# Mixture-of-experts layers of a one-core kernel: the rows of six sequences sorted by expert and run in 55 blocks of 128

## The reference

```python
scores = sigmoid(xf @ gate_w + bias)                # 4096 rows, 8 experts
top_scores, top_idx = top_k(scores, 2)
top_scores = top_scores / (sum(top_scores) + 1e-06)
w = zeros((T, E)).at[arange(T)[:, None], top_idx].add(top_scores)
up = einsum('th,ehi->tei', xf, up_w) + up_b         # h = 128, i = 512
hact = gelu(up)
eo = einsum('tei,eih->teh', hact, down_w) + down_b
combined = einsum('teh,te->th', eo * 0.1, w)
shared = (gelu(xf @ sw_up + sb_up) @ sw_down + sb_down) * 0.1
out = shared + combined
out = out / (max(abs(out), axis=-1) + 1e-06)        # then x = x + 0.5 * out
```

## Time and profile before

| | us |
|---|---|
| median of 3 runs | 1536.26 (1531.91 to 1538.03) |
| the profiled execution | 1536.07 |
| its span in the trace | 1534.3 |
| PE busy | 1386.0, 90% |
| DVE busy | 946.8, 62% |
| ACT busy | 800.9, 52% |
| POOL busy | 400.0, 26% |

### The profile page before, as it was taken

How to read it: one execution, slowest core, us unless ns; L and a number is a source line. 1 busy time by engine, 2 the same in 40 slices (tenths; PEclk the granted TensorE clock), 3 DMA queues, 4 the chain that set the end, 5 groups by cost and what they waited for, 6 DMA issues and landing times. The chain is left out here.

```text
span 1534.3 us, 24908 instructions
## 1 busy us (share of the span) xinstructions
PE 1386.0 (90%) x8338; PEld 725.6 (47%) x8338; DVE 946.8 (62%) x1898; ACT 800.9 (52%) x1465; POOL 400.0 (26%) x585
## 2 busy tenths in 40 slices
PE   2896999999999789799999996998998879999997
PEld 1771222222222268577777763221221257777776
DVE  5687788888889357441222274899999941222236
ACT  0221788888878624344434354656765444443432
POOL 3122233231231022300000003788887700000000
PEclk9995899999999989699999997899999979999999
DMA  4020222122221010000000002444444200000001
GB/s 95 2 84 1 73 74 74 41 72 75 73 73 33 2 19 2 1 16 16 1 16 17 1 1 64 150 152 137 142 146 145 96 8 9 17 17 1 17 15 42
DMA packets 81215, 77.44 MB, mean 50 GB/s; under 512 B 21005, under 2 KB 60377, under 8 KB 81113
## 3 DMA queue, kind: packets, MB, share of 16 engines
q1 hardware_dynamic: 78992, 75.85, 16.1%
q10 hardware_dynamic: 2120, 0.28, 0.2%
HBM read 55.78 MB, written 16.78 MB: 47 GB/s over the span
## 5 line engine op out<-in xcount | busy, mean ns | idle before, releaser
L1382 ACT ACTIVATE m_hidden<-m_pU,m_up_b 128x512 f32<-128x512 f32 x320 | 219.8, 687 | 265.6 <-PE m_pU L1531 265.3
L1190 DVE TENSOR_REDUCE at_nm<-at_mx 128x2 f32<-128x1024 f32 x256 | 304.0, 1220 | 40.7 <-PE at_mx L1033 39.3
L1538 PEld LDWEIGHTS m_pD<-m_down,m_hidden 128*128 128x128 f32 x2560 | 296.7, 192 | 32.5 <-issue 32.5
L1538 PE MATMUL m_pD<-m_down,m_hidden 128*128 128x128 f32 x2560 | 297.1, 275 | 0.0
L1136 ACT ACTIVATE at_probs<-at_ring 128x512 f32<-128x512 f32 x512 | 269.4, 605 | 47.5 <-PE at_ring L1045 45.8
L1531 PE MATMUL m_pU<-m_xT_all,m_up 128*128 128x512 f32 x640 | 291.2, 601 | 1.1 <-PEq L305 0.5
L1507 DVE TENSOR_TENSOR m_out_b<-m_pD,m_down_b 128x512 f32<-128x512 f32 x64 | 44.3, 692 | 288.3 <-PE m_pD L1538 288.3
L1531 PEld LDWEIGHTS m_pU<-m_xT_all,m_up 128*128 128x128 f32 x640 | 118.0, 193 | 123.7 <-issue 123.5
L2030 POOL TENSOR_TENSOR ss_hc<-ss_h,ss_c_all 128x512 f32<-128x512 f32 x128 | 161.9, 1273 | 53.3 <-DVE ss_h L2202 45.6
L1045 PE MATMUL at_ring<-at_qq,at_kk 51*128 51x512 bf16 x512 | 163.3, 386 | 7.0 <-ACT at_probs L1136 6.1
L1033 PE MATMUL at_mx<-at_kk,at_qq 48*128 48x512 bf16 x512 | 155.9, 398 | 13.5 <-DVE at_nm L1190 8.9
(11 more groups left out here) (285 smaller groups left out, 1525.6 us busy)
## 6 DMA issues: line engine op xcount, KB each, us to landing
ss_dtb<-ss_dt_rows SPq DMA_DIRECT2D x128, 256.0 KB
at_qq<-q_stack SPq DMA_DIRECT2D x64, 96.0 KB, 2.3
at_kk<-k_stack SPq DMA_DIRECT2D x64, 96.0 KB, 2.3
q_stack<-at_qs SPq DMA_DIRECT2D x8, 384.0 KB, 2.6
k_stack<-at_ks SPq DMA_DIRECT2D x8, 384.0 KB, 3.0
ss_stack<-ss_parts SPq DMA_DIRECT2D x96, 32.0 KB, 2.6
X<-in_L_attn_x_dram SPq DMA_DIRECT2D x8, 256.0 KB, 5.9
q_stack<-at_qs SPq DMA_DIRECT2D x8, 256.0 KB, 2.9
```

The costliest lines, as they stand in the source:

```text
L1190: dve.tensor_reduce(nm[group % 2][:, 2 * (pair % 2) + parity, 2 * half:2 * half + 2], mx[parity][:, :, :], AX.X, ALU.max, negate=True).the ...
L1382: act.activation(hidden[t % 2][:, k, :], pU[k][:, :], ACT.Gelu, bias=up_b[buf][:, k:k + 1]).then_inc(s.gelu_done, 1)
L1538: last = pe.matmul(pD[t % 2][:, c, :], hidden[t % 2][:, k, c * P:(c + 1) * P], down[buf][:, k, :], start=(k == 0), stop=(k == NI - 1))
```

## The change

Sequences 6 and 7 (`ND` = 2) still go through passes over the listed experts. The rows of sequences 0 to 5 (`HS` = 6) are sorted by expert:

1. The DVE chain also computes, for each of the 6144 pairs of row and expert, a place in a list in which each expert's rows start at a multiple of 128. Two extra matmuls (`ranks`, `totals`) count for it; they stand ahead of tile 1's ups in the shared pass and wait for 12 links of the chain.
2. POOL writes the normalised rows (130 floats: 128 values, a number and a weight) to these places in DRAM with 48 indirect DMAs of 128 rows, at most two at a time (`SCATTERS`). Between the 24th and the 25th it waits for all and rewrites the numbers and weights.
3. After the first two listed experts have done their two tiles, 55 blocks of 128 places (`HB`) run, unrolled, whether full or empty. For each, SP loads the rows (`xb`, a ring of 4) and the block's expert's `up` matrix (256 KB, `up_now`, a ring of 4). PE transposes the rows, and ACT copies the result. Then come four up matmuls of 128 columns, four gelus of 128x128, and four down matmuls from `down_all`, which holds all experts' `down` matrices. DVE adds the bias and multiplies by the weight, and POOL writes the result with an indirect DMA to the row's place in a second DRAM list (`put`). PE, ACT, DVE and SP read the block's expert from memory (`expert_at`, a TENSOR_LOAD).
4. When all 55 results have landed, SP loads them by sequence. The last two listed experts run their two tiles each. DVE adds the two results of each row and finishes sequences 0, 1 and 2 among the tiles of the third expert, 3, 4 and 5 behind the first tile of the fourth, then 6 and 7.
5. `silu(dve, lead, 0)` stands behind all of that.

The sorted list is filled with empty rows, for both MoE layers at once, during the first adapter layer (`fill_sorted`: two DMAs of 3.66 MB, in rows of 520 bytes, on SP's queue ahead of attention's first stores). The experts' biases are loaded in the second adapter layer. Behind the first MoE stand two more barriers of all engines, with the release of its semaphores.

```diff
+HS = 6
+ND = NB - HS
+HB = (2 * HT * P + E1 * (P - 1)) // P
+SCATTERS = 2
+X_BUFS, Y_BUFS, T_BUFS, U_BUFS = 4, 6, 3, 4
+FINISH_AT, SILU_AT = {0: (0,), 1: (1, 2), 2: (3, 4, 5)}, None
...
         def listed_experts(eng, expert, between):
             with eng.Fori(0, trips) as i:
                 expert(2 * i + 1, 1, 2 * i, i, None)
                 expert(2 * i + 2, 0, 2 * i + 1, i, None)
+            between(trips)
             expert(2 * trips + 1, 1, 2 * trips, trips, 0)
             expert(2 * trips + 2, 0, 2 * trips + 1, trips, 1)
...
+            def load_block(j):
+                if j >= X_BUFS:
+                    sp.wait_ge(s.y_ready, j - X_BUFS + 1)
+                sp.dma_start(xb[:, j % X_BUFS, :], sorted_rows[j * P:(j + 1) * P, :]).then_inc(xb_in[j % X_BUFS], 16)
+            def load_up(j):
+                e = expert_at(sp, j)
+                if j >= U_BUFS:
+                    sp.wait_ge(s.bup_done, j - U_BUFS + 1)
+                sp.dma_start(up_now[j % U_BUFS][:, :], ins["L1_ffn_up_w"][e]).then_inc(up_in[j % U_BUFS], 16)
...
-                    sp.wait_ge(s.down_done, NB * n - NB + 2)
+                sp.wait_ge(s.down_done, ND * n + (NB - 2 * ND) + 2)
...
+            expert(2 * trips + 1, 1, 2 * trips, trips, 0)
+            sp.wait_ge(s.blocks_ready, 1)
+            for i in range(SCATTERS):
+                sp.wait_ge(scattered[i], 16 * (2 * HT // SCATTERS))
+            for j in range(HB):
+                load_block(j)
+                load_up(j)
+            for i in range(Y_BUFS):
+                sp.wait_ge(y_out[i], 16 * len(range(i, HB, Y_BUFS)))
+            for b in range(HS):
+                load_results(b)
+                if b == 1:
+                    expert(2 * trips + 2, 0, 2 * trips + 1, trips, 1)
...
+            def scatter(k, t):
+                n = k * HT + t
+                if n >= SCATTERS:
+                    pool.wait_ge(scattered[n % SCATTERS], 16 * (n // SCATTERS))
+                pool.indirect_dma_start(sorted_rows, bass.IndirectOffsetOnAxis(ap=index[:, k, t:t + 1], axis=0),
+                                        v.rows[:, t, :], None, bounds_check=HB * P - 1, oob_is_err=False
+                                        ).then_inc(scattered[n % SCATTERS], 16)
...
+            def blocks(trips):
+                act.wait_ge(s.blocks_ready, 1)
+                take_turned(0)
+                take_turned(1)
...
+                for j in range(HB):
+                    after = expert_at(act, j + 1) if j + 1 < HB else None
+                    block_gelus(j, e)
+                    e = after
+                    if j + 2 < HB:
+                        take_turned(j + 2)
...
+                    dve.wait_ge(s.bdown_done, j + 1)
+                    dve.tensor_tensor(yt[j % 2][:, :], pD[j % 2][:, 0, :],
+                                      v.down_b[:, bass.ds(e, 1), :].rearrange("p a d -> p (a d)"), ALU.add
+                                      ).then_inc(s.y_taken, 1)
+                    dve.wait_ge(s.y_taken, j + 1)
+                    dve.tensor_scalar(y[j % Y_BUFS][:, :], yt[j % 2][:, :], xb[:, j % X_BUFS, WEIGHT:ROW], None, ALU.mult
+                                      ).then_inc(s.y_ready, 1)
...
+                for j in range(HB):
+                    if j + 2 < HB:
+                        turn(j + 2)
+                    if j + 1 < HB:
+                        block_up(j + 1)
+                    after = expert_at(pe, j + 1) if j + 1 < HB else None
+                    block_down(j, e)
+                    e = after
...
+            nc.all_engine_barrier()
+            nc.clear_and_free_semaphores(taken_once)
+            nc.all_engine_barrier()
```

More of the change, by code:

```diff
@@ L153, in scale_rows @@
     for c in range(NC):
-        last = act.activation(out[:, c, :], g.X[:, b, c, :], ACT.Identity, bias=t.shift[:, b, c:c + 1],
+        last = act.activation(out[:, c, 0:D], g.X[:, b, c, :], ACT.Identity, bias=t.shift[:, b, c:c + 1],
                               scale=g.rstd[:, b, c:c + 1])
@@ L296, in _, with adapter_ffn @@
             dve.wait_ge(st, 2 * half + 2)
-def adapter_ffn(nc, g, w, sem, tag, rows=None, lead=None, ins=None, ahead=None):
+def adapter_ffn(nc, g, w, sem, tag, rows=None, lead=None, ins=None, ahead=None, experts=None, places=None):
     s = record(**{n: sem(f"{tag}_{n}") for n in (
@@ L368, in _ @@
             take_rstd(pool, g, s.var, s.rstd, ones)
+            if lead is not None:
+                make_empty_row(pool, places)
             if rows is not None:
+                make_moe_constants(pool, experts)
                 for b in range(NB):
@@ L389, in transpose_rows @@
                 for c in range(NC):
-                    last = pe.transpose(pR[:, c, :], rows_xn[:, c, :], g.identf[:, :])
+                    last = pe.transpose(pR[:, c, :], experts.rows[:, b * NC + c, 0:D], g.identf[:, :])
                 last.then_inc(r.xT_done, 1)
@@ new lines, in moe_ffn @@
+        less, seat = sb("less", [P, E1, E1]), sb("seat", [P, E1, E1])
+        entry, listf = sb("entry", [1, E1, E1]), sb("listf", [1, E1])
+        pairsf, more = sb("pairsf", [1, 1]), sb("more", [1, 2])
+        down_all = sb("down_all", [P, E1, NI, D])
+        upto, place = sb("upto", [P, E1, HT]), sb("place", [P, E1, HT])
+        over, count = z2[:, 0:HT, :].rearrange("p t e -> p (t e)").rearrange("p (a t) -> p a t", a=E1), sb("count", [P, E1])
+        end, start = sb("end", [P, E1]), sb("start", [P, E1])
@@ new lines, in moe_ffn @@
+        at = sb("at", [P, 2, HT])
+        index = sb("index", [P, 2, HT], mybir.dt.int32)
+        expert_f = sb("expert_f", [1, HB])
+        expert_of = sb("expert_of", [1, HB], mybir.dt.int32)
+        hidden = [sb(f"hidden{i}", [P, NI, L]) for i in range(2)]
+        most = sb("most", [P, NT])
+        out_b = [sb(f"out_b{i}", [P, NC, D]) for i in range(2)]
+        xb = sb("xb", [P, X_BUFS, ROW])
+        passed = xb[0:1, :, :].rearrange("p i r -> p (i r)")[:, 0:HB * E1].rearrange("p (j e) -> p j e", j=HB)
@@ L1900, in scan_lead_act, with selective_scan @@
             front(act, q, s, 1, n)
-        for n in (5, 7):
-            back(act, s, 0, n)
-def selective_scan(nc, g, q, lead, m2, ins, sem, tag):
+    if t in (8, 9):
+        back(act, s, 0, 5 if t == 8 else 7)
+def selective_scan(nc, g, q, lead, m2, v, ins, sem, tag):
     s, r = lead, m2.s
```

773 lines of the change are left out of this document (491 added, 282 removed).

## The result

The changed kernel takes 1607.9 us (median of 4 runs, 1599.3 to 1611.5) against 1534.1 before (4 runs): a ratio of 1.047, 95% interval [1.044, 1.050]. 1630 was forecast, in a range of 1555 to 1740. Its profiled execution took 1608.5, with a span of 1606.7. I read all times of stages in such spans, and before's was 1534.3: the traces differ by 72.4 us, where the sum said 92.

What follows compares the result with a forecast made beforehand. The prediction took the MoE layers to be bound by PE's work. To the profiled 1536.1 us it added 38 (second MoE), 53 (first MoE) and 1 (fill), 1628, stated as 1630, range 1555 to 1740.

Steps and rivals of the forecast that it cites:

- the sum: Whole kernel: +38 us in the second MoE, +53 in the first and +1 for the fill, 92 in all.
- A block's period: In the blocks: time from one block to the next, T = (L + W) / 2, 3.0 us, bounds 2.4 and 3.6.
- L: In the blocks: an `xb` slot's way from block j-2's downs through DVE, SP and landing to the next transpose, 3.55 us.
- W: In the blocks: one PE iteration, from that transpose to the end of block j's downs, 2.45 us at clock 0.8.
- this sign of the prediction: In the blocks: the trace after would show a clock of about 0.8.
- Up to the blocks: From the MoE layer's start to the first block: shared pass, two passes with exposed loads, clock and late issue, 108 us.
- The scatters: Ahead of the blocks: 1.7 us each, ending at 98.9 us, covered by PE's 102.4; cover ends at 1.77.
- Behind the blocks: After the blocks: 50.5 us tail in the second MoE; 55.5 in the first, then `silu` 0.7, 19.7 and barriers 4.
- The fill: First adapter layer: 7.3 MB mostly lands before attention's first stores come up behind it, 1 us (0 to 8).
- POOL's `put`: Rival, in the blocks: a `put` over 3.0 us sets the period, 1695 to 1740 us; chance 0.28 with slow scatters.
- The rival that the ring doesn't bind: In the blocks: quick landing and a clock that stays up give T = 2.4, 65 us less, 1565; chance 0.13.
- The rival "not slower": Blocks run at PE's own pace, 1515 us at 1.95, break-even T = 2.15; chance 0.06 faster, 0.04 about the same.

Runs made afterwards that it cites:

- e1: The changed kernel with the `xb` ring 3 deep instead of 4 (the table `passed` moved to another buffer): 1974.3 us, 1.285 of before.
- e6: The changed kernel with the listed experts' weights loaded as soon as buffers are free, the last expert's ahead of the fourth block: 1582.1 us.
- e5: The changed kernel with one scatter in flight instead of two: 1731.8 us, 1.128 of before.
- e8: The changed kernel with `silu` moved ahead of finishes 4 to 7 in DVE's order: 1586.7 us.
- e3: The changed kernel with the `xb` ring 6 deep instead of 4: 1527.0 us, 0.994 of before.
- e2: The changed kernel with the `xb` ring 5 deep instead of 4: 1545.0 us, 1.006 of before.
- e12: The changed kernel with ring of 6, early expert loads and early `silu`, two scatters in flight: 1491.8 us, 0.971 of before.
- e9: The changed kernel with ring of 6, early expert loads, four scatters in flight and early `silu` together: 1546.0 us.
- e10: The changed kernel with four scatters in flight instead of two, nothing else: 1697.9 us.
- e11: The kernel of e9 run once more, unchanged, on another chip: 1544.6 us.
- e7: The kernel of e6 with four scatters in flight instead of two: 1547.3 us.
- e4: The changed kernel without the `up` matrix load and SP's read of the expert from the fifth block on, ring of 4: 1584.1 us.

## Why the prediction was right, point by point

Direction, place and mechanism were right; the sum was 20 us too high. That it came so near is partly luck: the blocks missed by -33.5 us, and the stages around them by some 18 the other way.

- **A block's period**, 3.0 forecast, 2.62 and 2.76 measured: the largest miss, -20.5 and -13.0 us. It was mis-sized twice. L was put at 3.55 and is 3.22: SP wakes in 0.03 us, not 0.3; the landing was taken at 2.4 and is 2.43. W was put at 2.45, by a clock of 0.8 taken from stages in which PE was about as busy. In the blocks PE was busy for 81 and 82%, and the granted clock was 0.98 and 0.95; this sign of the prediction failed. In e1 it did fall, to 0.66, with PE busy for 57%. L and W each came out 0.33 us smaller, and T takes half of each. ACT stayed below, with four gelus in 1.15 us, not 1.46.
- **Up to the blocks**, 108 forecast, 112.7 and 111.2 measured. The shared pass took 62.5 for 61.0. The exposed loads cost 5.8 and 6.0 us, as forecast, but behind each the ups ran at a lower clock, granted 0.83 and 0.73: 8.54 and 9.64 us where 7.03 do at full clock (e6), for which I had 2 us in all. `placed` came at 16.5, not 13.8.
- **The scatters**, 1.7 forecast between bounds of 1.05 and 2.24, 1.79 and 1.70 measured. The cover was said to end at 1.77, and the last scatter was to come before 100 us; it starts at 101.6 in the first MoE. It stayed hidden only because PE's part had grown too. e5 and e6 show how tight it is. The Trainium skill, DMA: Bandwidth & Descriptors, section on the anatomy of a GpSimd-issued DMA, gave by its fit an estimate of 2.15 us for such a DMA. The trace roughly agrees, with 2.3 us from issue to landing (e5). What was wrong was to take half of it, 1.1, for the pace: near 1 us of POOL's way to the next issue goes on top, and half of 3.28 is 1.64.
- **Behind the blocks**: tails of 58.4 and 56.0 us for 55.5 and 53.3. Behind `silu` 29.0 for 24.4: the last store is issued at 986.2, 23 us after `silu`'s end where 19.7 was forecast, and the barriers with the release take 5.3, not 4. e8 shows that 19 us of this are the place of `silu`.
- **The fill**: 1 us forecast, nothing measured. The scan was 3.5 us shorter, for which the sum had no term; in the traces of the variants it takes 292.2 to 298.8.
- **The rivals.** POOL's `put` takes 0.97 us and is idle for the rest: in e3 it keeps up with 1.91 us a block. By form, in its blocks:

```profile
L1524 POOL DMA_INDIRECT pair_rows<-m_y,m_y_id x50 | 48.6, 972 | 64.0 <-DVE m_y L1781 64.0
...
L1781 DVE TENSOR_SCALAR m_y<-m_yt,m_xb 128x128 f32<-128x128 f32 x51 | 14.7, 288 | 1.8
```

Neither is longer than in the blocks of the changed kernel (972 and 288). The Trainium skill, SBUF — State Buffer, "Who interferes with whom", would have DVE's operation hold up the descriptors; at this density, 0.29 us in 1.9, no row shows it. That is not a test of the rule, since `put` starts 0.9 us behind the operation of its own block. The rival that the ring doesn't bind gave T = 2.4; the first MoE's 2.62 lies nearer to that than to 3.0, but for another reason: the ring does bind, with a smaller L and W. The rival "not slower" named PE's own pace and a break-even of T = 2.15. Both hold: at T = 2.05 and 2.14, e2 is 0.6% over before. But it asked for a landing under 1.5 us, and the runs got there with more buffers at a landing of 2.6 and 2.8.

By the variants, then, the ring costs 81 us (e3), the exposed loads 26 as far as the scatters let them (e6), and the place of `silu` some 20 (e8). All three undone at once (e12) give 116, and the change is then 44 us faster than before on the same chip, of the 122 (2 x 61) that its PE work alone promised. The rest is still uncovered time around the blocks. In e12's first MoE they start 105.6 us into the layer, where PE has 58.5 + 28 us of work, and 69.4 us lie behind the last block's downs, where PE has 28 us of work.

## What stays open

Why four scatters in flight make all engines crawl in e9, e10 and e11 and not in e7. The allocations differ, and so do the programs: e7's chip was not used again. A queue that is full can't be read from the trace: in e10's window the DMA engines are busy for 15%. The Trainium skill, Runtime: NRT & Kernel Launch, "Instruction fetch mechanics", has each engine fetch its program through a queue of its own, mostly hidden. The traces show such fetches, in the window 668 to 728 of e10 and of e7:

```profile
q8 instruction: 1, 0.02, 0.1%
```

```profile
q8 instruction: 3, 0.05, 0.4%
```

In e10 queue 8 fetches 16 KB at 671 and next at 734, with 129 of PE's matmul records between them; in e7 134 records lie between its fetches at 670 and 692. So this queue keeps step with PE's work, and dozens of matmuls came late one by one with no fetch due: the rows speak against a starved fetch on PE. Nor would it explain why DVE learns of a finished matmul 22 us late. I tried neither three scatters in flight nor a pause between them. The 13 us that e7's blocks gained are open too. Ten of them lie in the second MoE, 2.58 us a block for 2.76: from issue to transpose single rows took up to 5.0 us there in the changed kernel, and at most 3.3 in e7.

## What to carry to other kernels

Before cutting PE's work into small units, draw the ring that feeds them: period = (time from release to refill + one unit of work) / (depth less the units that PE runs ahead). The landing grows with the traffic and single loads come late, so allow one buffer more than the quiet landing says; here two buffers of 520 bytes a partition were worth 81 us. When a long pass shrinks, look at each thing that it covered (weight loads, a side chain, an epilogue), and expect that removing one exposed wait shows the next: e6's gain ended at the scatters. And try a change with its neighbours as well as alone: four DMAs in flight instead of two were worth 35 us in one program (e7 against e6) and cost 90 in another, on another chip (e10), and 53 in a third, on one chip (e11 against e12).

## What the runs showed of the hardware

- A granted clock of 0.98 and 0.95 over 150 us in which PE was busy for 81 and 82%, 0.66 over 323 us in which it was busy for 57%.
- An indirect DMA of 128 rows of 520 bytes: 0.97 us on POOL (median), at least 0.30 to the next, 2.3 us from issue to landing. The pace is 3.28 us with one in flight, 1.7 to 1.8 with two, 1.4 with four.
- A 65 KB load lands in 1.8 us (median) with no 256 KB load beside it (e4) or with one every 6 us (e1), in 2.6 and 2.8 us with one every 2.1 and 1.9 us (e2, e3).
- SP, waiting for a semaphore, issues 0.03 us after DVE's operation has ended.
- Other engines can slow to a crawl beside back-to-back indirect DMAs, for a reason that these runs don't show: PE did 33 us of work in 60 where e7's did 60.
- Instruction fetches stand in the trace as DMAs of their own: queue 8 brings 16 KB for some 130 of PE's matmul records.
